# Inner products added ahead of the aggregation, and a third coefficient only where it is read

## What is computed

```python
def gn(v, G=32, eps=1e-05):
    g = v.reshape(B, G, C // G, H, W)
    m = mean(g, axis=(2, 3, 4)); s = var(g, axis=(2, 3, 4))
    return ((g - m) / sqrt(s + eps)).reshape(v.shape)

out = x + conv3x3(gn(x), sign(W))        # padding 1, 64 channels to 64
```

## Time and profile before

| | us |
|---|---|
| median of 3 runs | 202.27 (201.59 to 202.57) |
| profiled execution, first to last instruction (span) | 200.7 |
| PE busy in it | 191.2 (95%) |
| POOL, DVE, ACT busy | 166.7, 165.3, 149.7 |

### The profile page before, as it was taken

How to read it: one execution, slowest core, us unless ns; L and a number is a source line. 1 busy time by engine, 2 the same in 40 slices (tenths; PEclk the granted TensorE clock), 3 DMA queues, 4 the chain that set the end, 5 groups by cost and what they waited for, 6 DMA issues and landing times.

```text
span 200.7 us, 10042 instructions
## 1 busy us (share of the span) xinstructions
PE 191.2 (95%) x4482; PEld 168.4 (84%) x4482; DVE 165.3 (82%) x363; ACT 149.7 (75%) x142; POOL 166.7 (83%) x85
## 2 busy tenths in 40 slices
PE   1999999999999999999999999999999999999990
PEld 0478888879858988988999988899998999889990
DVE  2799999996999997799988779998779999627392
ACT  3185999799989289899909989972998999595000
POOL 1029786999999999999999997999999899999500
PEclk9999999999999999999999999999999999999999
DMA  6978977871787988868697887868887883906274
GB/s 216 362 217 292 331 246 252 289 209 44 306 243 291 297 316 282 282 248 278 242 301 296 275 327 276 325 228 321 326 241 296 266 319 152 381 13 238 116 283 175
DMA packets 18698, 52.17 MB, mean 260 GB/s; under 512 B 2080, under 2 KB 5024, under 8 KB 18656
## 3 DMA queue, kind: packets, MB, share of 16 engines
q1 hardware_dynamic: 18656, 51.54, 72.9%
HBM read 25.84 MB, written 25.69 MB: 257 GB/s over the span
## 4 chain that ended last, share of the span: by engine, by line
PE 65%; ACT 14%; DVE 13%; DMA 3%; issue 1%; SPq 0%; DVEq 0%; ACTq 0%
PE psum L738 65%; ACT halves L424 5%; DVE stats L500 5%; ACT xnorm L418 4%; DMA xbuf<-in_x_dram 3%; ACT moved L437 3%; DVE xbuf L570 2%; DVE xbuf L556 1%; DVE xbuf L580 1%; DVE own L508 1%; ACT line_halves L447 1%; ACT std L413 1%; DVE xbuf L544 1%; ACT lines_norm L451 1%; DVE halves L538 1%
## 5 line engine op out<-in xcount | busy, mean ns | idle before, releaser
L738 PE MATMUL psum<-halves,w_taps 64*64 64x385 f16 (+8 forms) x4140 | 183.4, 325 | 0.5 <-DVE halves L532 0.4
L738 PEld LDWEIGHTS psum<-halves,w_taps 64*64 64x64 f16 x4140 | 156.7, 107 | 19.3 <-ACT moved L437 0.9
L330 POOL TENSOR_TENSOR halves<-xnorm,halves 128x784 f16<-128x784 f32 (+5 forms) x35 | 91.6, 2637 | 20.0 <-ACT xnorm L418 19.7
L500 DVE BATCH_NORM_STATS2 stats<-xbuf 128x6 f32<-128x448 f32 x112 | 60.8, 613 | 4.3 <-DMA xbuf<-in_x_dram 4.1
L424 ACT ACTIVATE halves<-xbuf,coef 128x784 f16<-128x784 f32 (+5 forms) x35 | 50.7, 1449 | 3.0 <-DVE coef L525 2.8
L418 ACT ACTIVATE xnorm<-xbuf,coef 128x784 f32<-128x784 f32 (+5 forms) x35 | 50.5, 1443 | 0.0
L437 ACT ACTIVATE moved<-psum 64x784 f32<-64x784 f32 (+1 forms) x30 | 25.5, 850 | 7.9 <-PE psum L738 7.3
L345 POOL TENSOR_TENSOR xbuf<-xbuf,moved 128x784 f32<-128x784 f32 (+1 forms) x15 | 29.3, 1956 | 0.4 <-ACT moved L437 0.4
L570 DVE SCALAR_TENSOR_TENSOR xbuf<-psum,xbuf 64x784 f32<-64x784 f32 (+1 forms) x32 | 28.2, 881 | 1.0
L556 DVE SCALAR_TENSOR_TENSOR xbuf<-psum,xbuf 128x784 f32<-128x784 f32 x21 | 20.3, 967 | 7.6 <-PE psum L738 7.4
L371 POOL TENSOR_TENSOR line_halves<-lines_norm,line_halves 128x1512 f16<-128x1512 f32 (+1 forms) x10 | 20.9, 2120 | 0.5 <-ACT lines_norm L451 0.5
(11 more groups left out here) (36 smaller groups left out, 72.0 us busy)
## 6 DMA issues: line engine op xcount, KB each, us to landing
xbuf<-in_x_dram SPq DMA_DIRECT2D x48, 448.0 KB, 4.6
out_dram<-xbuf SPq DMA_DIRECT2D x43, 392.0 KB, 4.0
xbuf<-in_x_dram SPq DMA_DIRECT2D x16, 224.0 KB, 4.1
out_dram<-xbuf SPq DMA_DIRECT2D x5, 504.0 KB, 3.9
out_dram<-xbuf SPq DMA_DIRECT2D x5, 448.0 KB, 3.8
out_dram<-xbuf SPq DMA_DIRECT2D x5, 364.0 KB, 4.1
out_dram<-xbuf SPq DMA_DIRECT2D x5, 252.0 KB, 4.1
out_dram<-xbuf SPq DMA_DIRECT2D x1, 224.0 KB, 3.8
```

What stands on the lines that cost most here:

```text
L330: nc.gpsimd.tensor_tensor(at(halves[:, k % HRING, 1, :], a, b), at(xnorm[:, k % NRING, :], a, b), at(halves[:, k % HRING, 0, :], a, b), AL ...
L500: nc.vector.bn_stats(stats[:, n, :], xbuf[:, s, n * STAT:(n + 1) * STAT]).then_inc(blocks_ready, 1)
L738: mm = pe.matmul(outs[:, :, left:right], weights, ins[:, :, left + dx:right + dx], start=first_step, stop=last_step)
```

## The change

Two edits. In a WINOGRAD pair, `add_inner(k)` now stands ahead of `aggregate(k + 2)` in DVE's order. And `scale(k)` makes the third coefficient only for WINOGRAD pairs, counted on a semaphore of its own, `sum_ready`, so that `coef_ready` counts two a pair instead of three; ACT waits for `sum_ready` in `line_upper` ahead of the two activations that read it.

```diff
+        sum_ready = sem("sum_ready")
...
                 act.wait_ge(lines_made, 3 * n + 3)
+                act.wait_ge(sum_ready, n + 1)
                 nc.scalar.activation(line_halves[:, 0, SUM], lines[:, SUM], ACT.Identity,
...
-                act.wait_ge(coef_ready, 3 * (k + 1))
+                act.wait_ge(coef_ready, 2 * (k + 1))
...
-                dve.wait_ge(coef_ready, 3 * k + 1)
+                dve.wait_ge(coef_ready, 2 * k + 1)
                 nc.vector.tensor_scalar(coef[:, s, 1:2], own[:, 0:1], -1.0, coef[:, s, 0:1],
                                         ALU.mult, ALU.mult).then_inc(coef_ready, 1)
-                nc.vector.tensor_scalar(coef[:, s, 2:3], own[:, 0:1], -2.0, coef[:, s, 0:1],
-                                        ALU.mult, ALU.mult).then_inc(coef_ready, 1)
+                if k in WINOGRAD:
+                    nc.vector.tensor_scalar(coef[:, s, 2:3], own[:, 0:1], -2.0, coef[:, s, 0:1],
+                                            ALU.mult, ALU.mult).then_inc(sum_ready, 1)
...
+                if k in WINOGRAD:
+                    add_inner(k)
                 if k < NP - 2:
                     aggregate(k + 2)
-                if k in WINOGRAD:
-                    add_inner(k)
```

## The result

The changed kernel takes 208.63 us (median of 5 runs, 208.44 to 209.71), the kernel before 201.99 us (5 runs). The ratio is 1.0336, 95% interval 1.0309 to 1.0363: slower by 6.6 us, where 6.5 was forecast (208.8 us, with a range of 206.8 to 210.3). The profiled execution is the longest of the five, 209.71 us with a span of 207.9; the break that makes up its last microsecond comes under the last heading. Six of the executions behind the times of this document took over 1.5% longer than the fastest of their kernel and are left out of the ratios and intervals, though not of the medians; one of them, 256.23 us at a granted clock of 0.76, is the profiled one of the kernel with the copy first, which therefore ran a second time.

The account below looks back on a forecast made before the run. The PE was taken to bound the kernel, busy 191.2 of 200.7 us. Delays of 1.12 + 1.77 + 1.78 + 1.81 = 6.5 us on a 202.27 us median gave 208.8 us, range 206.8 to 210.3.

Parts of the forecast that it names:

- The floor set by product 1: In WINOGRAD pairs on DVE, the inner products end 1.48 us after the PE's first product-0 matmul.
- The terms: PE delays from ACT's late copies: 1.12 us in pair 3, 1.77 in 6, 1.78 in 9, 1.81 in 12.
- The signs named in advance: Changed profile: four PE waits for ACT's copies near 2 us, deviations awaiting DVE, 5 third-coefficient instructions, span 207.2 us.
- The parts listed for the range: Pair 3 and shuffle: 208.3 to 209.7; run spread: 0.7 below, 0.3 above; smaller terms: low end 206.8 us.
- Pair 3: DVE, not the PE, sets the products' start; dropped coefficients bring it 0.48 us earlier, deviation 1.12 us later.
- The two floors: Pair 3's inner products end at about 57.24 us as set by DVE, 57.17 as set by the PE.
- The small waits of before: In the kernel before, PE weight loads wait four times for ACT's copies, 0.9 us in all, 0.19 in pair 7.
- No slack at all: ACT's copies behind the deviation: a microsecond's delay of that deviation is a microsecond of the PE.
- The freed banks: Rival: the products' earlier-freed banks decide, not the copy; 201.7 us, or 200.8 with other waits gone; chance 0.06.
- taken back: Rival: the PE runs the next pair's home steps during away waits, covering half of each stall; 205.5 us, chance 0.06.
- The clock: Rival: the PE's clock falls in the four new stalls, 3 us lost per stall, 220.8 us; chance 0.04.

Follow-up runs that it names:

- the kernel with the copy first: Changed kernel with ACT's copy out of PSUM put ahead of the deviation; 201.41 us, ratio 0.9979, and 201.56 us, ratio 0.9963, when run again.
- order edit alone: Kernel before with only the inner products put ahead of the aggregation on DVE, third coefficient still made for all 16 pairs; 208.78 us, ratio 1.0353.
- coefficient edit alone: Changed kernel with the aggregation put back ahead of the inner products, keeping only the third-coefficient edit; 201.96 us, ratio 1.0000.
- the swap alone: Kernel before with ACT's copy out of PSUM put ahead of the deviation; 201.58 us, ratio 1.0000.
- the products parted: Changed kernel with product 2's two additions ahead of the aggregation and product 1's two behind it; 203.45 us, ratio 1.0064.
- the wait alone: Kernel before with ACT's deviation after pairs 3, 6, 9 and 12 also waiting until the inner products are added; 208.19 us, ratio 1.0300.
- two pairs: Changed kernel with the inner products ahead of the aggregation in pairs 6 and 12 only; 205.41 us, ratio 1.0158.

## Why the prediction was right

*The floor set by product 1.* Predicted: the products end 1.48 us after the first product-0 matmul. In the changed kernel that matmul starts at 91.23 in pair 6 (the rows are those of pairs 3, 6 and 9, in the form of the earlier trace rows):

```profile
55.26 0.37 PE L741 MATMUL psum<-line_halves,w_taps 64*64 64x504 f16 x1
...
91.23 0.38 PE L741 MATMUL psum<-line_halves,w_taps 64*64 64x504 f16 x2
...
127.13 0.38 PE L741 MATMUL psum<-line_halves,w_taps 64*64 64x504 f16 x2
```

and the products end at 90.16 + 2.55 = 92.71, which is 1.48 us. The deviation follows 0.72 us later (0.73 predicted). Pair 14, where no aggregation follows, was a true picture of what pair 6 would become.

*The terms.* They can be read from the starts of these matmuls, against the earlier trace rows. From pair 6 to pair 9 the changed kernel takes 127.13 - 91.23 = 35.90 us and the kernel before 34.16: 1.74 lost, where 1.77 was predicted. From pair 3 to pair 6 it takes 35.97 against 34.72: 1.25 lost in pair 3, where the prediction had 1.24, less 0.12 for an earlier start. In this profile the stretch behind pair 9 holds the further break of the last heading, so for pairs 9 and 12 I go by the order edit alone, which loses 1.74 and 1.73 us in them. Together that is 6.5 us, and the medians differ by 6.6. The signs named in advance are there too: the deviations wait for DVE, and 5 instructions are left at the third coefficient.

*Slips that changed nothing.* 54.82 + 2.44 is 57.26 and not 57.24. The deviation was to end 93.02 - 92.51 = 0.5 us after the products of before, not 0.6. The parts listed for the range add up to 206.4 to 210.0, not 206.8 to 210.3. And the level of 208.8 started from 202.27 us, the median of three runs, which with five is 201.99.

*Pair 3, right in size and wrong in its reason.* I had DVE set the time of the products there. In the changed kernel DVE arrives early and waits for the PE too:

```profile
52.98 0.98 DVE L547 SCALAR_TENSOR_TENSOR xbuf<-psum,xbuf 128x392 f32<-128x392 f32 x2
54.26 2.55 DVE L590 SCALAR_TENSOR_TENSOR xbuf<-psum,xbuf 128x504 f32<-128x504 f32 x4 [0.30 <-PE psum L741]
```

Its home add starts at 52.98 instead of 54.34, 1.4 us earlier and not 0.48. Part of that is the start of this execution: the first real matmul is at 11.80 instead of 12.35. Counted from that matmul, DVE is 0.81 us earlier here, 0.48 in the coefficient edit alone and not at all in the order edit alone: the dropped coefficients do it, and why they bring more here than by themselves stays open. The two floors were only 0.07 us apart in the prediction, so the size held.

*The small waits of before were mis-sized.* I read the weight loads' waits of 0.19 us as time lost by the PE, and so expected 0.9 and 1.3 us of gain from the two swaps on ACT. The medians showed 0.2 for the swap alone, with a ratio of 1.0000, and 0.4 and 0.5 for the changed kernel with it. The starts of the matmuls tell it better. From pair 6 to pair 9 the kernel before takes 124.69 - 90.53 = 34.16 us, with a weight load's wait of 0.19 in it. The changed kernel with the copy first, where that wait is gone, takes just as long:

```profile
89.23 0.38 PE L741 MATMUL psum<-line_halves,w_taps 64*64 64x504 f16 x2
...
123.39 0.38 PE L741 MATMUL psum<-line_halves,w_taps 64*64 64x504 f16 x2
```

So the wait of 0.19 us cost the PE nothing. In the other kernels the same stretch is 34.63 us with a wait of 0.69 (the products parted), 35.72 with 1.78 (the wait alone) and 35.90 with 1.97 (the changed kernel): 0.47, 1.56 and 1.74 us lost. Each time the first 0.22 us or so of the weight loads' wait is not lost by the matmuls.

The whole stream agrees. In the tile view of psum, a row gives the count of the tap matmuls, their shortest, median and longest duration in ns, and their first and last start in us. The changed kernel, then the changed kernel with the copy first:

```profile
L741 PE MATMUL psum<-halves,w_taps x4140: 209/327/373, 11.8 to 202.8; 64*64 64x385 f16 x121, 64*64 64x392 f16 x22, 64*64 64x330 f16 x13, 64*64 64x336 f16 x12
```

```profile
L741 PE MATMUL psum<-halves,w_taps x4140: 209/327/373, 11.5 to 194.4; 64*64 64x385 f16 x119, 64*64 64x392 f16 x26, 64*64 64x336 f16 x13, 64*64 64x330 f16 x12
```

The same row in every profile gives the length of the stream:

| kernel | first to last tap matmul, us |
|---|---|
| before | 12.4 to 195.7: 183.3 |
| changed | 11.8 to 202.8: 191.0 |
| order edit alone | 11.8 to 202.0: 190.2 |
| the wait alone | 11.4 to 201.1: 189.7 |
| two pairs | 11.3 to 197.9: 186.6 |
| products parted | 12.1 to 196.8: 184.7 |
| before, copy first | 11.4 to 194.5: 183.1 |
| coefficient edit alone | 12.0 to 195.0: 183.0 |
| changed, copy first | 11.5 to 194.4: 182.9 |

By the one profile of each, the kernel before was only 0.4 us above the shortest stream. The waits of the PE itself showed none for ACT in it, while in the changed kernel they read:

```profile
PE psum L741 <- ACT moved L438: 6.2, 4, 1.5
```

That is less than the 6.5 us lost by starts; the ends of matmuls are modelled, so a break between an end and a start is rough. That the forecast was still right has a simple reason: the 0.19 us of before had already used up nearly all of the 0.22 that are not lost, so of the delay added to each wait all but some hundredths reaches the PE. "No slack at all" was right to that degree.

*The rivals.* The freed banks brought at most some tenths (the coefficient edit alone, and the copy first). Next to nothing was taken back: against the product-0 matmul of pair 6 the deviation came 1.76 us later than before, and the PE lost 1.74. The clock did not fall. Windows on the stall ahead of pair 7 and on the 2 us behind it (busy of PE, PEld, DVE, ACT, POOL; clock; DMA; GB/s):

```profile
93.50:95.60 2.10, 0.61 (x14) 0.18 (x4) 1.82 (x7) 2.05 (x3) 1.56 (x1) 1.00 0.95 337
95.60:97.60 2.00, 1.95 (x50) 1.77 (x54) 1.91 (x4) 1.98 (x2) 1.93 (x1) 1.00 0.71 284
```

The granted clock is listed as 1.00 (2.4 GHz) in the stall and behind it. That alone would not settle it, for the stretch of the slow fillers in the kernel before, 6.08 / 17 = 0.36 us a round of four, is listed as 1.00 too:

```profile
4.20:12.40 8.20, 7.84 (x106) 4.41 (x110) 6.53 (x18) 2.09 (x6) 0.00 (x0) 1.00 0.93 329
```

The pace settles it: behind the stall 50 matmuls in 2.00 us are 0.16 us a round, and from the first away load of pair 4 to the first product-0 matmul of pair 6 both kernels take 31.48 us (59.75 to 91.23, and before 59.05 to 90.53). The Trainium skill, "TensorE: Matmul & The Clock Gate", section "A second HAM failure mode: psum-queue depth-cycling", tells of frequent small gaps that make the clock swing. Four breaks of under 2 us, some 36 us apart, showed no such swing; frequent ones were not tried here.

## What to carry to other kernels

Before a step is moved back on one engine, look at who waits for it on another, and then at what stands behind that waiter in its own program order: here an activation of 0.29 us held up a copy that had nothing to do with it, and the copy held the bank that the bounding engine needed. When a wait must become later, swap it behind the work that does not depend on it; here that took away the whole loss, and left 0.2 to 0.4% of gain. And to see what a stall costs the PE, compare the starts of the same two matmuls with and without it: here the waits of the weight loads showed 0.22 us too much each, and the waits of the PE itself too little.

## Not expected

The profiled execution of the changed kernel has one more break, 1.1 us in its weight loads from 144.5 and 0.75 us in its matmuls, ended by nothing that the profile shows:

```profile
145.64 1.68 PE L741 MATMUL psum<-halves,w_taps 64*64 64x385 f16 x35 [0.75 <-issue]
```

That execution took 209.71 us, the other four 208.44 to 208.91, so the break most likely belongs to this execution and not to the change; the eight other profiles that the table compares have none like it. Its cause stays open. The start is uncertain as well: over these nine profiles the first real matmul begins between 11.3 and 12.4 us, which is more than the whole gain of the best version.
